# Queries turned whole two sequences ahead and stacked through DRAM, and the residual's load issued three exponentials later

## The chip, the cores and the metric

One core of a Trainium2 chip runs the kernel. The metric is the device time of one execution in microseconds; of several runs the median counts. The chip's engines run side by side and meet only at semaphores: TensorE (PE: matmuls, PEld: its weight loads), VectorE (DVE), ScalarE (ACT), GpSimd (POOL) and SyncE (SP). SyncE and ScalarE also issue the transfers (DMA), each from a queue of its own.

## The reference

64 sequences of 256 rows and 512 columns go through a cross-attention block and a gated mixing block. All is float32.

```python
def _L0_xattn_ref(q, k, v, ffn_w, ffn_b):           # 16 heads of 32
    qs = relu(q.reshape(bs, ts, h, hd)); ks = relu(...); vs = relu(...)
    att = einsum('bthf,byhf->bhty', qs, ks)
    att = softmax(att / sqrt(hd), axis=-1)
    out = einsum('bhty,byhf->bhtf', att, vs).reshape(bs, ts, -1)
    return relu(out @ ffn_w.T + ffn_b)

def _L0_ffn_ref(x, W_r, W_k, W_v, mu_r, mu_k):
    x_prev = concatenate([zeros, x[:, :-1]], axis=1)
    xr = mu_r * x + (1 - mu_r) * x_prev; xk = mu_k * x + (1 - mu_k) * x_prev
    r = sigmoid(xr @ W_r.T); k_act = square(relu(xk @ W_k.T))
    return r * (k_act @ W_v.T)

x = x + tanh(g_xattn[0]) * _L0_xattn_ref(layernorm(x), ctx, ctx, ffn_w, ffn_b)
x = x + tanh(g_ffn[0]) * _L0_ffn_ref(layernorm(x), W_r, W_k, W_v, mu_r, mu_k)
```

## The kernel before

A sequence is the unit of work. All weights stay in SBUF. Each engine has its own program, written out by hand: a function `iteration(i, par)` that lists its operations for sequence i and, beside them, those of i - 1, i - 2, i + 1 and i + 2, so that four sequences are under way at once. `pipeline` runs it for a few i as plain code, for most in a loop of two, and for the last ones plainly again. Within an engine this written order is the order of execution; waits on semaphores stand in the helpers.

**Precision.** A float32 operand is split into a high part (rounded to float32r) and a low part. Dense products take three matmuls (`product`, L951). Queries and keys are stacked for it: 96 partitions hold three parts of a head's 32 features, queries as high, high, low and keys as high, low, high, so that one matmul gives the whole score.

**Heads.** The 16 heads go in four groups of four, c = 0 to 3. For each head n, `scores` (L906) gives scores with queries down the partitions; VectorE takes each row's negated maximum (`head_max`, L699) into `m_nat`. When a group's four heads have theirs, `turn_m` (L884) turns them into `tp_bank`, `copy_m` (L708) copies them to `m_t`, and SyncE moves them (`move_m`, L279) as one row, partition 96, into `q_st`. `shifted_scores` (L918) then gives the scores the other way round with the maximum already taken off, ScalarE takes the exponential (`exponent`, L496) into `probs`, and `values` (L932) and `denominators` (L944) use them. The first shifted scores of a group wait for the group's row:

```python
if g == 0:
    pe.wait_ge(m_moved[c % 2], 16 * (2 * b + c // 2 + 1))
```

**Queries.** x is normalised in `x_ln`; ScalarE writes two high parts (`q_high`, L469 and L470) and VectorE the low part (`q_low`, L674) of a half of the sequence into `q_nat`. TensorE turns them, four heads of 96 columns at a time (`turn_q`, L875), and ScalarE copies each turn into `q_st` (`q_stack`, L477): eight turns and eight copies for a sequence.

**Keys.** They come turned from the host. `load_k` (L250) fetches those of i + 2; `k_halve` (L485) on ScalarE and `k_low` (L682) on VectorE split them; `write_k` (L258) writes both parts to `k_dram`, and `stack_k` (L270, L272) reads a group from there into `k_st`, in the next iteration.

**SyncE's queue.** It issues, in this order: `stack_k(i, 3)`, `store(i - 3)` (L301), `move_m(i, 1)`, `write_o`, `read_o` (L294: the attention's output through DRAM), `load_k(i + 2)`, `stack_k(i + 1, 0)`, `move_m(i, 2)`, and so on to `write_k(i + 2)`. A wait in it holds back all that follows.

**Residual.** `load_x1` (L453) brings x once more, into the buffer that `store` empties, so it waits for a store to have landed. ScalarE issues it between exponentials 1 and 2.

## Time and profile before

| | |
|---|---|
| median of 3 runs | 2981.95 us (2980.19 to 2983.81) |
| the profiled execution: its time, and its span | 2980.25 us, 2978.4 us |
| TensorE busy | 2860.3 us, 96% |
| VectorE, ScalarE, GpSimd busy | 2330.1, 1564.3, 1045.4 us |
| mean granted clock of TensorE | 0.993 of full |
| moved by DMA | 408.56 MB, mean 137 GB/s |
| busy share of the DMA engines: SyncE's queue, ScalarE's | 39.6%, 7.3% |

The span runs from the first to the last instruction. Busy time of TensorE is modelled from starts and shapes, so 96% says only that a matmul was under way. L numbers are lines of the kernel before.

### The profile page before, as it was taken

What the parts mean: (1) busy time and instruction counts of PE and PEld (TensorE: products, weight loads), DVE (VectorE), ACT (ScalarE), POOL (GpSimd) and SP (SyncE); (2) the same over time, 40 slices, a digit from 0 to 9 for tenths busy, and PEclk for the clock granted to TensorE, in tenths of its full rate; (3) what the DMA queues carried; (4) which work ended last, traced back from release to release, by engine and by line L of the source; (5) the groups of instructions that cost most, each with busy time, mean ns of one, the idle gap of its engine ahead of it and who ended that gap; (6) DMA issues with size and microseconds to landing.
All of it is one profiled execution on the core that took longest, in us unless ns stands there. A gap on an engine that the chain in (4) does not pass through costs nothing.

```text
span 2978.4 us, 71298 instructions
## 1 busy us (share of the span) xinstructions
PE 2860.3 (96%) x23168; PEld 2190.6 (74%) x23168; DVE 2330.1 (78%) x4175; ACT 1564.3 (53%) x2828; POOL 1045.4 (35%) x902
## 2 busy tenths in 40 slices
PE   3899999999999999999999999999999999999998
PEld 2677777777777777777777777777777777777776
DVE  5777877878878878878877877877878778788774
ACT  4445555555455455555555555555555555554552
POOL 0233333333343343333333333333333333333434
PEclk9899999999999999999999999999999999999999
DMA  5544445445445445445445445455455454454431
GB/s 168 150 122 140 144 124 155 140 127 155 135 131 156 137 131 154 133 137 150 131 142 149 128 143 153 120 149 152 120 152 146 124 152 142 124 156 137 130 109 41
DMA packets 405258, 408.56 MB, mean 137 GB/s; under 512 B 164577, under 2 KB 329441, under 8 KB 405218
## 3 DMA queue, kind: packets, MB, share of 16 engines
q1 hardware_dynamic: 352994, 340.92, 39.6%
q10 hardware_dynamic: 52224, 67.12, 7.3%
q8 instruction: 24, 0.39, 0.1%
q14 instruction: 16, 0.13, 0.0%
HBM read 272.64 MB, written 134.22 MB: 137 GB/s over the span
## 4 chain that ended last, share of the span: by engine, by line
PE 59%; DVE 16%; DMA 10%; SPq 7%; issue 5%; ACT 1%; ACTq 1%; DVEq 0%; POOL 0%; POOLq 0%
PE bank L951 29%; DMA out_dram<-x 8%; PE bank L918 7%; PE bank L932 6%; PE bank L906 5%; PE bank L944 4%; DVE m_nat L699 4%; DVE o_val L718 4%; SPq L272 3%; DVE st L652 3%; DVE k_raw L682 2%; PE bank L893 2%; PE bank L875 2%; SPq L258 2%; SPq L270 2%
## 5 line engine op out<-in xcount | busy, mean ns | idle before, releaser
L496 ACT ACTIVATE probs<-bank 128x512 f32<-128x512 f32 x1024 | 596.4, 594 | 455.7 <-PE bank L918 228.1
L699 DVE TENSOR_REDUCE m_nat<-bank 128x2 fp32r<-128x512 f32 x1024 | 695.4, 685 | 107.4 <-PE bank L906 106.7
L477 ACT ACTIVATE q_st<-bank 96x512 fp32r<-96x512 f32 x512 | 304.1, 594 | 718.9 <-PE bank L875 718.8
L918 PE MATMUL bank<-q_st,k_st 97*128 97x256 f32 x2048 | 449.9, 301 | 64.2 <-ACT probs L496 47.4
L718 DVE RECIPROCAL o_val<-bank 128x256 f32<-128x256 f32 x256 | 449.1, 1754 | 56.1 <-PE bank L944 51.7
L918 PEld LDWEIGHTS bank<-q_st,k_st 97*128 97x128 f32 x2048 | 341.8, 191 | 153.8 <-issue 58.5
L906 PE MATMUL bank<-k_st,q_st 96*128 96x256 f32 x2048 | 431.6, 293 | 7.4 <-DMA k_st<-k_dram 4.8
L397 POOL TENSOR_TENSOR xm<-xm 128x512 f32<-128x512 f32 x128 | 133.3, 1041 | 787.2 <-ACT xm L540 787.2
L906 PEld LDWEIGHTS bank<-k_st,q_st 96*128 96x128 f32 x2048 | 358.2, 192 | 59.8 <-issue 6.2
L708 DVE CAST m_t<-bank 4x256 fp32r<-4x256 f32 x256 | 105.1, 411 | 285.5 <-PE bank L884 285.4
L364 POOL TENSOR_TENSOR o_lo<-o_mv,o_hi 128x512 fp32r<-128x512 f32 x128 | 164.8, 1287 | 430.0 <-ACT o_hi L503 430.0
L951 PE MATMUL bank<-xk_hi,w_hi 128*128 128x256 f32 x1024 | 298.5, 292 | 0.0
L951 PE MATMUL bank<-xk_lo,w_hi 128*128 128x256 f32 x1024 | 286.5, 280 | 0.0
L951 PE MATMUL bank<-xk_hi,w_lo 128*128 128x256 f32 x1024 | 286.4, 280 | 0.0
L932 PE MATMUL bank<-probs,v_pos 128*32 128x256 f32 x4096 | 276.3, 388 | 0.6 <-DVE o_val L720 0.6
L944 PE MATMUL bank<-probs,ones_r 128*32 128x256 f32 x4096 | 276.3, 388 | 0.0
L875 PEld LDWEIGHTS bank<-ident_r,q_nat 128*96 128x96 f32 x2048 | 192.6, 127 | 71.0 <-issue 51.9
L875 PE MATMUL bank<-ident_r,q_nat 128*96 128x128 f32 x2048 | 218.6, 230 | 23.8 <-DVE q_nat L674 20.5
L382 POOL TENSOR_TENSOR xk_lo<-xm,xk_hi 128x512 fp32r<-128x512 f32 x128 | 164.5, 1286 | 215.0 <-ACT xk_hi L527 183.6
L356 POOL TENSOR_TENSOR rstd<-ve,mhalf 128x1 f32<-128x1 f32 x128 | 69.2, 541 | 422.8 <-DVE ve L736 422.8
L951 PE MATMUL bank<-w_hi,xr_hi 128*128 128x512 f32 x512 | 208.4, 407 | 4.2 <-POOL xr_lo L390 4.2
L951 PE MATMUL bank<-w_hi,o_hi 128*128 128x512 f32 x512 | 207.8, 406 | 4.7 <-POOL o_lo L364 4.7
(90 smaller groups left out, 6026.6 us busy)
## 6 DMA issues: line engine op xcount, KB each, us to landing
k_st<-k_dram SPq DMA_DIRECT2D x256, 256.0 KB, 3.6
k_raw<-ctx_t_dram SPq DMA_DIRECT2D x256, 128.0 KB, 3.0
x_ln<-x_dram SPq DMA_DIRECT2D x256, 128.0 KB
k_dram<-k_high SPq DMA_DIRECT2D x64, 512.0 KB, 3.0
k_dram<-k_raw SPq DMA_DIRECT2D x64, 512.0 KB, 4.5
k_st<-k_dram SPq DMA_DIRECT2D x256, 128.0 KB, 3.5
o_dram<-o_val SPq DMA_DIRECT2D x256, 128.0 KB, 1.7
o_mv<-o_dram SPq DMA_DIRECT2D x512, 64.0 KB, 2.2
```

Source lines behind the costliest of these rows:

```text
L364: nc.gpsimd.tensor_tensor(by_tile(o_lo, u), o_mv[:, :, :].rearrange("p g (k a) -> p k g a", k=KC), by_tile(o_hi, u).bitcast(F32), ALU.subt ...
L382: nc.gpsimd.tensor_tensor(xk_lo[:, part, :], xm[:, part, :], xk_hi[:, part, :].bitcast(F32), ALU.subtract).then_inc(xk_lo_ready, 1)
L477: nc.scalar.activation(q_st[0:QK, c, :, P * u:P * u + P], tp_bank[0:QK, :].rearrange("p (g t) -> p g t", g=GR), ACT.Copy).then_inc(q_stack ...
L496: nc.scalar.activation(probs[:, n // GR % 2, n % GR, :, :].rearrange("p v t -> p (v t)"), st_bank[n % 2][:, :], ACT.Exp, scale=SCALE).then ...
L699: nc.vector.tensor_reduce(m_nat[:, c % 2, :, n % GR:n % GR + 1], s_bank[n % 2][:, :].rearrange("p (u y) -> p u y", u=NU), AX_X, ALU.max, n ...
L718: nc.vector.reciprocal(o_val[:, :], pv_bank[:, T:2 * T]).then_inc(rden_ready, 1)
L875: mm = nc.tensor.transpose(tp_bank[0:QK, P * g:P * g + P].bitcast(F32R), q_nat[:, u, GR * c + g, :, :], ident_r[:, :])
L906: mm = nc.tensor.matmul(s_bank[n % 2][:, T * u:T * u + T], q_st[0:QK, c, g, P * u:P * u + P], k_st[0:QK, c, g, :], start=True, stop=True)
L918: mm = nc.tensor.matmul(st_bank[n % 2][:, T * v:T * v + T], k_st[0:ST, c, g, P * v:P * v + P], q_st[0:ST, c, g, :], start=True, stop=True)
L932: nc.tensor.matmul(pv_bank[HD * g:HD * g + HD, 0:T], v_pos[:, v, HD * h:HD * h + HD], probs[:, c % 2, g, v, :], start=(v == 0), stop=(v == ...
L944: mm = nc.tensor.matmul(pv_bank[HD * g:HD * g + HD, T:2 * T], ones_r[:, 0:HD].bitcast(F32), moving, start=(n == 0), stop=(n == len(sums) - 1))
L951: mm = nc.tensor.matmul(dst, lhs[a], rhs[c], start=first and n == 0, stop=last and n == 2)
```

## The change

It does four things.

- Queries of i + 2 are normalised by VectorE into `q_nat`, its columns reordered so that a group's features lie as (feature, head). TensorE turns them whole, not split: two turns of four 128-column blocks in plain float32. ScalarE copies each turn with a relu into `q_raw`, then rounds `q_raw` into `q_high`; VectorE subtracts.
- SyncE writes both parts to a new DRAM tensor `q_dram` and reads each group from there into `q_st`, three parts of 32 partitions, in two transfers a group, next to those of the keys.
- `load_x1` is issued between exponentials 4 and 5.
- x is loaded, and its statistics taken, three sequences ahead instead of two; the pipeline starts at i = -3.

```diff
+            def write_q(b, par):
+                if on(b):
+                    sp.wait_ge(q_hi_ready, b + 1)
+                    sp.wait_ge(q_lo_ready, b + 1)
+                    for half, tile in enumerate((q_high, q_raw)):
+                        sp.dma_start(q_dram[par, :, half].rearrange("c f g t -> (f g) c t"),
+                                     tile[:, :, :]).then_inc(q_written, 16)
+            def stack_q(b, c, par):
+                if on(b):
+                    sp.dma_start(q_st[0:HD, c, :, :].bitcast(F32), q_dram[par, c, 0]).then_inc(q_stacked[c], 16)
+                    sp.dma_start(q_st[HD:QK, c, :, :].bitcast(F32),
+                                 q_dram[par, c].rearrange("h f g t -> (h f) g t")).then_inc(q_stacked[c], 16)
...
             def iteration(i, par):
                 stack_k(i, 3, par)
+                stack_q(i, 3, par)
                 store(i - 3, 1 - par)
                 move_m(i, 1)
...
                 keys_written(i + 1)
                 load_k(i + 2)
+                queries_written(i + 1)
                 stack_k(i + 1, 0, 1 - par)
+                stack_q(i + 1, 0, 1 - par)
                 move_m(i, 2)
...
                 write_k(i + 2, par)
+                write_q(i + 2, par)
...
-            def q_stack(b, c, u):
+            def q_copy(b, u):
                 if on(b):
+                    act.wait_ge(q_turned, NU * b + u + 1)
+                    after(act, q_written, 32 * b)
+                    nc.scalar.activation(q_raw[:, :, P * u:P * u + P],
+                                         tp_bank[:, :].rearrange("p (c t) -> p c t", c=CH),
+                                         ACT.Relu).then_inc(q_copied, 1)
...
+            def turn_q(b, u, *users):
+                if on(b):
+                    pe.wait_ge(x_normed, NU * b + u + 1)
                     freed(*users)
+                    for c in range(CH):
+                        mm = nc.tensor.transpose(tp_bank[:, P * c:P * c + P], q_nat[:, u, c, :],
+                                                 ident_r[:, :].bitcast(F32))
                     mm.then_inc(q_turned, 1)
...
                 head_max(i + 1, 1)
+                q_low(i + 2)
```

SyncE's queue, from the end of one iteration into the next. Before:

```order
L258 DMA k_dram<-k_high 128x4x256
L258 DMA k_dram<-k_raw 128x4x256
L194 REGISTER_ALU
L270 DMA k_st<-k_dram 64x1024
L272 DMA k_st<-k_dram 32x1024
L300 REGISTER_ALU
L301 ISA
L301 DMA out_dram<-x 128x2x512
L278 REGISTER_ALU
L279 DMA q_st<-m_t 1x4x256
```

The same place with the change, from the last write of the keys on:

```order
L281 DMA q_dram<-q_high 128x4x256
L281 DMA q_dram<-q_raw 128x4x256
L199 REGISTER_ALU
L272 DMA k_st<-k_dram 64x1024
L274 DMA k_st<-k_dram 32x1024
L291 DMA q_st<-q_dram 32x1024
L292 DMA q_st<-q_dram 64x1024
L321 REGISTER_ALU
L322 ISA
L322 DMA out_dram<-x 128x2x512
L299 REGISTER_ALU
L300 DMA q_st<-m_t 1x4x256
```

Two writes and one pair of reads of the queries now stand between the writes of the keys and the store; the move of `m_t` follows the store in both.

ScalarE around the load of the residual, `x<-x_dram` (the exponentials are L496 before, L518 with the change). Before, from head 0 to head 2:

```order
L496 ACTIVATE probs<-bank 128x512
L489 REGISTER_ALU
L496 ACTIVATE probs<-bank 128x512
L474 REGISTER_ALU
L477 ACTIVATE q_st<-bank 96x4x128
L453 REGISTER_ALU
L453 DMA x<-x_dram 128x2x512
L489 REGISTER_ALU
L496 ACTIVATE probs<-bank 128x512
L540 ACTIVATE xm<-bank 128x512
```

With the change, from head 3 on:

```order
L518 ACTIVATE probs<-bank 128x512
L511 REGISTER_ALU
L518 ACTIVATE probs<-bank 128x512
L199 REGISTER_ALU
L480 REGISTER_ALU
L480 DMA x<-x_dram 128x2x512
L562 ACTIVATE xm<-bank 128x512
L492 REGISTER_ALU
L199 REGISTER_ALU
L494 ACTIVATE q_raw<-bank 128x4x128
L523 ISA
L525 ACTIVATE o_hi<-o_mv 128x4x128
```

The load of the residual stood ahead of the exponential of head 2 and now stands behind that of head 4, and the copies into `q_st` are gone from between.

## Rows read from the trace of the kernel before

**Rows 1.** The page: the span, and TensorE's busy time, share and instructions.

```profile
span 2978.4 us, 71298 instructions
...
PE 2860.3 (96%) x23168; PEld 2190.6 (74%) x23168; DVE 2330.1 (78%) x4175; ACT 1564.3 (53%) x2828; POOL 1045.4 (35%) x902
```

**Rows 2.** Waits from 500 to 2500 us: us in total, times, longest us.

```profile
ACT probs L496 <- DMA out_dram<-x: 158.4, 45, 3.8
...
PE bank L918 <- ACT probs L496: 32.4, 45, 1.0
```

**Rows 3.** The chain that ended last, one sequence: start, us, what.

```profile
1403.54 0.51 PE bank L918 x2
...
1409.15 0.21 PE bank L884 x2
...
1415.16 0.24 PE bank L918 x2
...
1430.46 0.23 PE bank L884 x2
...
1439.41 0.39 SPq L258
...
1443.08 4.14 DMA out_dram<-x
...
1448.63 0.47 PE bank L918 x2
```

**Rows 4.** Timeline of SyncE's queue: start us, us.

```profile
1402.57 1.87 SPq L294 DMA_DIRECT2D o_mv<-o_dram  x4
1404.73 2.85 SPq L250 DMA_DIRECT2D k_raw<-ctx_t_dram  x4
...
1440.46 1.01 SPq L270 DMA_DIRECT2D k_st<-k_dram  x1
...
1443.59 0.62 SPq L279 DMA_DIRECT2D q_st<-m_t  x1
```

**Rows 5.** Timeline of TensorE: in brackets the idle time before, and its releaser.

```profile
1448.63 0.47 PE L918 MATMUL bank<-q_st,k_st 97*128 97x256 f32 x2 [0.78 <-ACT probs L496]
```

**Rows 6.** Busy time by stretch, with PEclk, DMA share and GB/s at the end.

```profile
1397.00:1398.00 1.00, 1.00 (x11) 1.00 (x10) 1.00 (x1) 0.00 (x0) 0.00 (x0) 1.00 0.99 345
...
1404.00:1411.00 7.00, 7.00 (x61) 4.70 (x61) 3.49 (x6) 6.12 (x12) 4.27 (x4) 1.00 0.88 259
...
1440.00:1447.00 7.00, 7.00 (x75) 6.02 (x68) 6.77 (x12) 0.59 (x1) 0.00 (x0) 1.00 0.95 300
```

**Rows 7.** The chain again: products, and turns of queries (L875) and of xn (L893).

```profile
1415.40 0.70 PE bank L951 x3
...
1416.34 0.25 PE bank L875 x4
1416.59 0.76 PE bank L951 x3
...
1419.28 0.59 PE bank L893 x4
```

**Rows 8.** Groups by line: busy us, mean ns, idle before and releaser.

```profile
L477 ACT ACTIVATE q_st<-bank 96x512 fp32r<-96x512 f32 x512 | 304.1, 594 | 718.9 <-PE bank L875 718.8
...
L674 DVE SCALAR_TENSOR_TENSOR q_nat<-x_ln,q_nat 128x512 fp32r<-128x512 f32 x128 | 99.1, 775 | 108.1 <-ACT q_nat L470 108.1
...
L682 DVE SCALAR_TENSOR_TENSOR k_raw<-k_raw,k_high 128x1024 fp32r<-128x1024 f32 x64 | 79.1, 1236 | 0.0
```

**Rows 9.** Timeline of VectorE at the turn of 1430.46.

```profile
1430.80 0.41 DVE L708 CAST m_t<-bank 4x256 fp32r<-4x256 f32 x1 [2.07 <-PE bank L884]
```

**Rows 10.** An early standstill: timeline of TensorE, the stretch behind it, the chain.

```profile
182.74 0.47 PE L918 MATMUL bank<-q_st,k_st 97*128 97x256 f32 x2 [2.43 <-ACT probs L496]
...
183.42:186.83 3.41, 3.41 (x11) 2.75 (x11) 1.39 (x2) 3.41 (x8) 1.49 (x2) 0.50 1.13 306
...
183.71 1.28 PE bank L951 x3
```

More of the change, by code:

```diff
@@ L139, in flamingo_block @@
         q_turned = sem("q_turned")
-        q_stacked = sem("q_stacked")
+        q_copied = sem("q_copied")
+        q_written = sem("q_written")
+        q_stacked = [sem(f"q_stacked{c}") for c in range(CH)]
         v_ready = sem("v_ready")
@@ L207, in pipeline @@
         def pipeline(eng, iteration):
-            for i in range(-2, 4):
+            for i in range(-3, 4):
                 iteration(i, i % 2)
-            with eng.Fori(6, NB // 2 + 3) as pair:
+            with eng.Fori(6, NB // 2 + 2) as pair:
                 iteration(pair * 2 - 8, 0)
                 iteration(pair * 2 - 7, 1)
-            for i in range(NB - 2, NB + 3):
+            for i in range(NB - 4, NB + 3):
                 iteration(i, i % 2)
@@ L314, in iteration @@
                 stack_k(i + 1, 1, 1 - par)
-                load_x(i + 2)
+                stack_q(i + 1, 1, 1 - par)
+                load_x(i + 3)
                 move_m(i, 3)
@@ L318, in iteration @@
                 stack_k(i + 1, 2, 1 - par)
+                stack_q(i + 1, 2, 1 - par)
                 move_m(i + 1, 0)
@@ L580, in iteration @@
                 exponent(i, 4)
+                load_x1(i - 1, 1 - par)
                 kt_relu(i - 2, 1)
-                q_high(i + 1, 1)
+                q_copy(i + 2, 0)
                 o_high(i - 1, 1)
@@ L1059, in iteration @@
                 values(i - 1, 3)
-                turn(1)
+                turn(0)
                 denominators(i - 1, 3)
@@ L1064, in iteration @@
                 dense(0, 3)
-                turn(2)
                 shifted_scores(i, 2)
@@ L1072, in iteration @@
                 shifted_scores(i, 3)
-                turn(3)
                 dense(1, 2)
@@ L1081, in iteration @@
                 dense(2, 1)
+                turn(1)
                 shifted_scores(i, 5)
@@ L1099, in iteration @@
                 scores(i, 14)
-                turn(6)
                 dense(3, 3)
@@ L1105, in iteration @@
                 scores(i, 15)
-                turn(7)
                 dense(4, 1)
@@ L1119, in iteration @@
                 denominators(i, 1)
-                turn(10)
+                turn(6)
                 scores(i + 1, 1)
@@ L1127, in iteration @@
                 dense(5, 3)
-                turn(11)
                 shifted_scores(i, 12)
@@ L1137, in iteration @@
                 values(i, 2)
-                turn(12)
+                turn(7)
                 scores(i + 1, 4)
@@ L1145, in iteration @@
                 denominators(i, 2)
-                turn(13)
                 dense(7, 1)
```

100 lines of the change are left out of this document (39 added, 61 removed).

## The prediction, made before the changed kernel ran

> **What bounds the kernel now.** I read the engines' totals first, then who waits for whom in the steady part, then the chain that ended last, then the queue on that chain. The totals [rows 1] show TensorE busy for 2860.3 of 2978.4 us. That reads like a kernel bound by matmuls, but the busy figure says nothing of who sets the pace. The waits between 500 and 2500 us [rows 2] hold one odd entry: ScalarE waits 45 times, up to 3.8 us, for the store of an output to land, and L918 on TensorE waits 45 times for an exponential. Once in every sequence, then.
>
> The chain through one sequence [rows 3] shows why. Name the shifted scores of head 4 (L918, first of group 1) S4. They start at 1403.54 and, one sequence on, at 1448.63: a period of 45.09 us. Between them the chain goes in three legs:
> - A: TensorE from S4 to its turn of the maxima of the next sequence's group 0 (L884 at 1430.46): 26.92 us without a hole that counts.
> - B: VectorE from there through its statistics, a reciprocal and k_low (L682) until SyncE can issue write_k (L258) at 1439.41: 8.95 us, one operation behind the other, while TensorE runs ahead.
> - C: the queue of SyncE: write_k, stack_k, then the store at 1443.08, which lands 4.14 us later, at 1447.22. Only then can ScalarE issue load_x1 (L453) and go on to the exponential that S4 waits for.
>
> TensorE idled 0.78 us before S4 [rows 5], so it was ready at 1447.85. In leg C the DMA engines are full: 0.95 busy at 300 GB/s from 1440 to 1447, with no room in it [rows 6]. So leg C is a matter of bytes: 1 MB of keys, 384 KB of stacks, 512 KB of output. And behind the store in the same queue stands the move of m for group 1 (L279, issued at 1443.59) [rows 4]. It carries the row that S4 needs. The profile gives no landing for it; it is 4 KB behind the store in one queue, so I put it at the store's landing, 1447.2. It can't be later than 1448.63, or S4 would not have run.
>
> **The change on TensorE.** Per sequence, eight turns of four matmuls (L875) go, and two turns of the form of L893 come. In the chain a turn of L875 takes 0.25 us and slows the product behind it from 0.70 to 0.76 [rows 7]: 0.31 us, eight times 2.5. L893 takes 0.59 [rows 7], twice 1.2. TensorE gains 1.3 us. Where: two of the eight lie between k_low's end and S4, two more between the turn at 1430.46 and k_low's end, four in leg A. The two new ones lie both in leg A. So leg A keeps its length (4 x 0.31 against 2 x 0.59) but for 0.1 us of a wait for ScalarE that goes: 26.8 us. The gain is all before S4, where TensorE is ready at 1447.85 - 4 x 0.31 = 1446.6, and there it waits.
>
> **On ScalarE and VectorE.** ScalarE loses eight copies of 594 ns (L477) [rows 8] and the four halvings of q_high, and gets two copies of that size and one halving of twice the size: some 5 us of work less in 45. What it has left to do is waited for nowhere in the chain but behind the store, so nothing comes of that by itself. VectorE swaps two operations of 775 ns for one like k_low, 1236 ns [rows 8]. It stands after head_max(i + 1, 1), ahead of the turn at 1430.46, where VectorE idles 2.07 us [rows 9]; 1.24 us fits. If that cover were gone, leg B would start later by what exceeds it. Leg B's own operations stay as they are: 8.95 us.
>
> **load_x1 three exponentials later.** That takes the wait for the store away from ScalarE: the load now stands behind exponential 4, thus behind S4, when the store has long landed. But S4 then waits for the next thing in line, the row of m behind the same store. At an unchanged queue the period would be 26.8 + 8.95 + 7.8 (1447.22 less 1439.41) = 43.6 us, a gain of 1.5 us and no more.
>
> **What is put into the queue.** Per sequence two writes of 512 KB and four pairs of stacks of 384 KB: 2.5 MB. What counts is what stands ahead of the row of m. As the order of the queue shows, after write_k come both writes of q, and after stack_k(3) comes stack_q(3), all ahead of the store and of m. That is 1.05 + 0.39 = 1.44 MB in a stretch that is full already. At leg C's 300 GB/s it takes 4.8 us; at the pace of the fastest microsecond, 345 GB/s [rows 6], 4.2. I take 4.7, near the mean, since the mix is the same (1 KB pieces written, 4 KB read). Issuing costs nothing: the stack's issue takes 1.01 us and the move's 0.62 [rows 4], and four more of that size still run ahead of the bytes. A small extra: load_v, which stood behind ScalarE's wait, now falls into this stretch, 128 KB or 0.4 us; I leave that to the upper end. The Trainium skill (DMA: Bandwidth & Descriptors, Specifications) puts the limit of HBM for a core at about 358 GB/s. By that figure the 1.44 MB could not take less than 4.0 us, and the forecast would be 0.7 us a sequence lower; the stretch's own 300 GB/s is what I go by.
>
> **The rest of the queue.** The nearest danger is the row of m for group 2, issued behind read_o (1.87 us), load_k (2.85 us) [rows 4], stack_k(0) and now stack_q(0), 1.1 us each: about 7.5 us behind S4. Its turn (L884) comes 5.6 us behind S4 today [rows 3], about 6.2 with a new turn ahead of it. The DMA engines are 0.88 busy over the 7 us behind S4 [rows 6]; with 1.3 us for stack_q(0) that is 7.5 us of bytes, done by some 9.5 us behind S4, and the row by 10.5. The shifted scores of head 8 come 11.6 us behind S4 [rows 3], then 12.2. So no second wait, by under 2 us. The other two stacks of q fall behind that, where nothing is near.
>
> **The period after.** 26.8 + 8.95 + 7.8 + 4.7 = 48.3 us, against 45.1: +3.2. From 1430.46 TensorE needs 16.1 us until it is ready for S4, so it stands still for 48.3 - 26.8 - 16.1 = 5.4 us in every sequence.
>
> **The clock.** Early in this trace there is such a standstill: at 182.74 S4 starts after 2.43 us of idling [rows 10]. From 183.42 to 186.83 the granted clock is 0.50, the 1.2 GHz level, and three products take 1.28 us [rows 10] in place of 0.70 [rows 7]. Work at half the clock for 3.41 us loses 1.7 us. A standstill of 5.4 us should do that too. From below: nothing, if the clock held after all. From above: two such stretches, 3.4 us. I take one, 1.7, since one is what the row shows. The Trainium skill (TensorE: Matmul & The Clock Gate, What's actually happening) says that the throttled state is the default and that activity releases it; by that rule the fall comes back in every sequence that has the standstill, and by the row it came at least once.
>
> **The sum.** 3.2 + 1.7 = 4.9 us a sequence. A sequence has all of it when a later one's queries are written ahead of its row of m: all but the first and the last few, I count 61. 299 us. The few early sequences that stood and slowed before already had part of it, about -8. The longer fill (queries through DRAM before the first score) about +5, an estimate from the same legs. The profiled execution took 2980.25 us beside a span of 2978.4 [rows 1], within 2 us of the median 2981.95. 2980 + 299 - 3 = 3276; I say 3275.
>
> **Rivals.**
> - *Stall and clock as forecast*: 3185 to 3370, likeliest 3275. Chance 0.63.
> - *Stall, but the clock holds*: +3.2, or +2.7 with 4.2 us for the bytes: 2980 + 61 x 2.7 to 3.2 = 3145 to 3175. Against it: 182.74 [rows 10], a shorter standstill. Chance 0.15.
> - *More waits than that*: the margin at head 8 breaks, or there are two stretches of slow clock and load_v's bytes as well, 2 us more a sequence: 3275 + 122 = 3397 and up. Chance 0.08.
> - *Faster: the row of m isn't held up.* If it lands before TensorE is ready, TensorE itself is the period: 26.8 + 16.1 = 42.9 us, 2.2 less, 61 times 134: 2845. If it still waits for the store as today, 43.6: 61 x 1.5 = 92 less, 2890. Either needs the added bytes to pass beside the others, or m's few pieces to pass them. From 1.5 us of added delay on nothing is left (43.6 + 1.5 = 45.1), and I count 4.7. For it: 1.3 us of matmuls and a wait of up to 3.8 us [rows 2] really go. Against: DMA engines without room in this stretch [rows 6]. Chance 0.11.
> - *The two cancel*, within 0.2% (6 us): needs just this 1.5 us. Chance 0.03.
>
> 0.2% is about what a measurement of this kernel tells from no change. Slower: 0.63 + 0.15 + 0.08 = 0.86; same 0.03; faster 0.11. The range goes from 3140 (bytes at their fastest, no slow clock) to 3375 (the bytes at their slowest and load_v's with them, 3.3 + 0.4, and most of a second slow stretch, 2.8: 6.5 x 61 = 395); that leaves out the fast case and the worst one, some 0.2.
>
> **What would show it.** L918's idle time before S4 put down to the move of m (q_st<-m_t), 4 to 6 us, once a sequence; the wait of ScalarE for out_dram gone; DMA full for about 12 us in a row after k_low; the granted clock at half for a few us behind each S4; S4 to S4 near 50 us. TensorE's busy share falls from 96% [rows 1] to below 90%, though it has less to do. Wrong would be: S4 unwaited and a period near 43; or the bytes of q gone through in under 2 us; or a new wait elsewhere, on scores for q_st or in the products for o_hi.

## The result, and the profile after

The changed kernel takes 3377.32 us (median of 4 runs, 3374.70 to 3382.67), against 2981.07 us (4 runs, 2977.55 to 2983.81) for the kernel before on the same chip: 1.133 times, 95% interval 1.131 to 1.135. That is 396 us more, where the forecast had 293. It lies 2 us above the top of the range.

The page of the changed kernel, to be held against [rows 1]. In the lines of its groups stand busy us, mean ns, then idle us ahead and its releaser:

```profile
span 3376.4 us, 66228 instructions
...
PE 2912.3 (86%) x21632; PEld 2220.3 (66%) x21632; DVE 2396.3 (71%) x4111; ACT 1329.0 (39%) x2252; POOL 1042.2 (31%) x902
...
L933 PE MATMUL bank<-q_st,k_st 97*128 97x256 f32 x2048 | 471.3, 314 | 325.5 <-DMA q_st<-m_t 325.5
```

TensorE has 86% where 96% stood, and 325.5 us of idling before one line: L933, which was L918 before, put down to the move of m. Yet its busy time is longer than before though it does less: part of it runs at half the clock. The waits between 500 and 2900 us (us in total, times, longest us):

```profile
ACT probs L518 <- PE bank L933: 1094.3, 563, 8.1
...
PE bank L933 <- DMA q_st<-m_t: 227.0, 47, 5.2
...
PE bank L921 <- DVE m_nat L716: 38.1, 47, 0.9
```

Once a sequence TensorE stands for the row of m, 4.8 us on average, where it stood 45 times for an exponential [rows 2]. ScalarE's wait for the store is gone. New besides is that TensorE waits for VectorE's maxima, 0.8 us a sequence before the scores of head 10 (the last line) and 0.3 us before their turn (L899: 15.2 us, 47 times); the kernel before has neither wait in its steady part. S4 is found early and late in TensorE's timeline, in brackets the idle time before it:

```profile
428.62 0.80 PE L933 MATMUL bank<-q_st,k_st 97*128 97x256 f32 x2 [5.14 <-DMA q_st<-m_t]
...
2527.61 0.79 PE L933 MATMUL bank<-q_st,k_st 97*128 97x256 f32 x2 [4.70 <-DMA q_st<-m_t]
```

There are 41 sequences between them: 51.2 us each. The store of an output gives the same count more handily, since SyncE issues it once a sequence. The row of all 64 (ns, then start of the first and of the last):

```profile
L322 SPq DMA_DIRECT2D out_dram<-x x64: 400/406/592, 217.7 to 3373.1; - x64
```

In the kernel before they start at 175.2 and 2975.1. From the seventh to the 57th it takes 2560.1 us after (524.83 to 3084.97) and 2249.9 before (453.73 to 2703.66): 51.20 and 45.00 us a sequence. So of the 398 us between the two spans 42 fall before the first store, and the rest is 6.2 us a sequence. One sequence in the chain that ended last (start us, us, what), beside [rows 3]:

```profile
1498.12 5.40 DMA q_st<-m_t
1503.64 0.79 PE bank L933 x2
...
1504.86 1.28 PE bank L966 x3
...
1507.85 0.85 PE bank L890 x4
...
1532.39 0.23 PE bank L899 x2
...
1540.06 1.22 DVE k_raw L699
...
1545.39 0.74 SPq L272
1546.17 1.33 SPq L274
...
1549.44 5.01 DMA q_st<-m_t
1554.49 0.80 PE bank L933 x2
```

The products behind S4 take 1.28 us for three, the half-clock price, in place of 0.70 [rows 7]. The chain ends in the queue, as forecast. SyncE's timeline at that place (start us, us of issuing), against [rows 4]:

```profile
1541.35 0.39 SPq L260 DMA_DIRECT2D k_dram<-k_high  x1
...
1542.39 0.99 SPq L281 DMA_DIRECT2D q_dram<-q_high  x1
1543.44 1.30 SPq L281 DMA_DIRECT2D q_dram<-q_raw  x1
...
1547.54 0.46 SPq L291 DMA_DIRECT2D q_st<-q_dram  x1
...
1548.92 0.41 SPq L322 DMA_DIRECT2D out_dram<-x  x1
1549.44 0.66 SPq L300 DMA_DIRECT2D q_st<-m_t  x1
```

From write_k's issue at 1541.35 to S4 at 1554.49 are 13.14 us. In that stretch, from ScalarE's queue, falls also the transfer of load_v, 128 KB:

```profile
1545.70 0.39 ACTq L486 DMA_DIRECT2D v_pos<-ctx_dram  x1
```

Two stretches of the same kernel, the first over the full DMA engines, the second over the slow clock (PEclk, DMA share and GB/s are the last three columns):

```profile
1542.00:1554.00 12.00, 7.17 (x64) 6.08 (x64) 9.42 (x15) 1.69 (x3) 1.24 (x1) 0.98 0.99 303
1553.60:1560.40 6.80, 5.91 (x19) 5.03 (x20) 0.69 (x1) 1.85 (x4) 1.04 (x1) 0.50 0.71 197
```

The DMA engines are full for 12 us at 303 GB/s, the pace the forecast took from [rows 6]. And the clock stands at 0.50, the 1.2 GHz level, for 6.8 us around S4: twice the 3.41 us of the early standstill [rows 10]. All 47 slow stretches between 500 and 2900 us are that long, one in each sequence.

### The profile page after: what moved, and what is told of

The parts are those of the page before. It is cut to its first block, busy times and chain, and to the rows that moved or that the text cites. A ratio compares the mean times of both kernels' runs of the same rounds, so it can differ in the third digit from the quotient of the medians.

```text
span 3376.4 us, 66228 instructions
## 1 busy us (share of the span) xinstructions
PE 2912.3 (86%) x21632; PEld 2220.3 (66%) x21632; DVE 2396.3 (71%) x4111; ACT 1329.0 (39%) x2252; POOL 1042.2 (31%) x902
## 4 chain that ended last, share of the span: by engine, by line
PE 61%; DVE 15%; DMA 11%; SPq 8%; issue 4%; DVEq 0%; POOL 0%; ACT 0%; POOLq 0%; ACTq 0%
PE bank L966 31%; DMA q_st<-m_t 10%; PE bank L933 7%; PE bank L959 6%; PE bank L947 6%; PE bank L921 5%; DVE m_nat L716 4%; DVE o_val L735 3%; SPq L274 3%; PE bank L890 2%; DVE k_raw L699 2%; DVE st L667 2%; PE bank L908 2%; PE bank L899 2%; SPq L272 1%
## 5 line engine op out<-in xcount | busy, mean ns | idle before, releaser
L518 ACT ACTIVATE probs<-bank 128x512 f32<-128x512 f32 x1024 | 610.1, 596 | 1501.4 <-PE bank L933 1501.2
L933 PE MATMUL bank<-q_st,k_st 97*128 97x256 f32 x2048 | 471.3, 314 | 325.5 <-DMA q_st<-m_t 325.5
L933 PEld LDWEIGHTS bank<-q_st,k_st 97*128 97x128 f32 x2048 | 379.0, 207 | 412.3 <-DMA q_st<-m_t 198.5
L921 PE MATMUL bank<-k_st,q_st 96*128 96x256 f32 x2048 | 450.8, 303 | 61.3 <-DVE m_nat L716 54.6
L921 PEld LDWEIGHTS bank<-k_st,q_st 96*128 96x128 f32 x2048 | 374.1, 200 | 134.1 <-DVE m_nat L716 68.9
L424 POOL TENSOR_TENSOR xm<-xm 128x512 f32<-128x512 f32 x128 | 146.5, 1145 | 973.9 <-ACT xm L562 973.9
L966 PE MATMUL bank<-w_hi,o_hi 128*128 128x512 f32 x512 | 240.9, 471 | 3.4 <-POOL o_lo L391 3.4
L966 PE MATMUL bank<-w_hi,o_lo 128*128 128x512 f32 x512 | 232.9, 455 | 0.0
L966 PE MATMUL bank<-w_lo,o_hi 128*128 128x512 f32 x512 | 230.0, 449 | 0.0
L966 PEld LDWEIGHTS bank<-xk_hi,w_hi 128*128 128x128 f32 x1024 | 193.3, 189 | 26.0 <-issue 25.9
L966 PE MATMUL bank<-w_hi,ka_hi 128*128 128x512 f32 x512 | 210.1, 410 | 0.0
```

What stands on the lines that cost most here:

```text
L424: nc.gpsimd.tensor_tensor(part, part, part, ALU.mult).then_inc(ka_ready, 1)
L518: nc.scalar.activation(probs[:, n // GR % 2, n % GR, :, :].rearrange("p v t -> p (v t)"), st_bank[n % 2][:, :], ACT.Exp, scale=SCALE).then ...
L921: mm = nc.tensor.matmul(s_bank[n % 2][:, T * u:T * u + T], q_st[0:QK, c, g, P * u:P * u + P], k_st[0:QK, c, g, :], start=True, stop=True)
L933: mm = nc.tensor.matmul(st_bank[n % 2][:, T * v:T * v + T], k_st[0:ST, c, g, P * v:P * v + P], q_st[0:ST, c, g, :], start=True, stop=True)
L966: mm = nc.tensor.matmul(dst, lhs[a], rhs[c], start=first and n == 0, stop=last and n == 2)
```

## The experiments

"After" is the changed kernel. The table has for each the median in us and its runs; the ratio to the kernel before on the same chip, with its 95% interval; from its profile the start of the first store and the time of a sequence (seventh to 57th store, over 50), in us; and the mean granted clock.

| | us | ratio | first store | a sequence | clock |
|---|---|---|---|---|---|
| before | 2981.07 (2977.55 to 2983.81) | | 175.2 | 45.00 | 0.993 |
| after | 3377.32 (3374.70 to 3382.67) | 1.133 (1.131 to 1.135) | 217.7 | 51.20 | 0.934 |
| e1 | 3066.05 (3060.74 to 3072.55) | 1.028 (1.026 to 1.030) | 207.4 | 46.07 | 0.977 |
| e2 | 3276.49 (3266.31 to 3289.66) | 1.101 (1.097 to 1.105) | 212.4 | 49.31 | 0.961 |
| e3 | 3258.49 (3252.00 to 3263.53) | 1.093 (1.091 to 1.095) | 214.4 | 49.08 | 0.993 |
| e4 | 2936.17 (2933.43 to 2938.08) | 0.985 (0.983 to 0.987) | 178.1 | 44.38 | 0.997 |
| e5 | 3017.12 (3013.74 to 3020.28) | 1.013 (1.011 to 1.014) | 201.2 | 45.31 | 0.994 |
| e6 | 3380.92 (3379.38 to 3381.07) | 1.135 (1.133 to 1.137) | 217.6 | 51.20 | 0.932 |
| e7 | 2945.99 (2942.17 to 2951.82) | 0.990 (0.988 to 0.991) | 172.0 | 44.59 | 0.997 |
| e8 | 3406.80 (3400.76 to 3409.46) | 1.143 (1.141 to 1.145) | 220.3 | 51.69 | 0.929 |
| e9 | 3382.58 (3380.59 to 3388.88) | 1.136 (1.134 to 1.138) | 215.5 | 51.19 | 0.933 |
| e10 | 2919.54 (2917.95 to 2925.01) | 0.981 (0.979 to 0.982) | 203.9 | 43.59 | 0.994 |
| e11 | 2889.29 (2888.49 to 2890.71) | 0.970 (0.969 to 0.971) | 173.5 | 43.64 | 0.996 |
| e12 | 3438.24 (3431.12 to 3443.88) | 1.154 (1.151 to 1.156) | 218.3 | 52.24 | 0.978 |
| e13 | 2936.01 (2935.18 to 2940.07) | 0.986 (0.984 to 0.987) | 202.5 | 43.87 | 0.993 |
| e14 | 2940.32 (2927.69 to 2955.68) | 0.987 (0.985 to 0.990) | 206.2 | 43.85 | 0.991 |
| e15 | 3149.14 (3141.69 to 3152.47) | 1.058 (1.056 to 1.059) | 207.3 | 47.34 | 0.993 |

The prediction's three legs, measured in the traces: A from S4 to the start of the turn of the maxima, B from there to the issue of write_k, C from there to the next S4. These are means in us over 48 sequences, from the ninth's S4 to the 57th's. The fourth column is TensorE's idle time right before S4, the last when the store of the output lands, counted from the issue of write_k (in the queue it stands ahead of the row of m for group 1, except in e10 and e11).

| | A | B | C | idle before S4 | store landed |
|---|---|---|---|---|---|
| before | 26.82 | 9.03 | 9.15 | 0.72 | 7.80 |
| after | 28.71 | 9.03 | 13.47 | 4.83 | 13.39 |
| e1 | 27.06 | 9.03 | 9.98 | 1.34 | 10.07 |
| e3 | 26.71 | 9.02 | 13.35 | 0.63 | 13.35 |
| e6 | 28.16 | 9.02 | 14.01 | 6.15 | 12.65 |
| e8 | 27.98 | 9.02 | 14.71 | 6.07 | 14.52 |
| e9 | 28.76 | 9.03 | 13.40 | 4.77 | 13.34 |
| e10 | 26.09 | 9.03 | 8.48 | 0.00 | 10.74 |
| e11 | 26.35 | 9.03 | 8.27 | 0.00 | 8.40 |
| e15 | 26.67 | 9.03 | 11.65 | 0.17 | 11.61 |

**Where the bytes stand: e1, e9, e15.** e1 is after with both writes of q ahead of write_o(i, 2) and write_k:

```diff
                 read_o(i, 0)
+                write_q(i + 2, par)
                 write_o(i, 2)
                 write_k(i + 2, par)
-                write_q(i + 2, par)
```

> The changed kernel with the two writes of the queries issued ahead of write_o(i, 2), where the DMA engines are idle, instead of behind write_k. Nothing else differs. Theory (what counts is the bytes that stand ahead of the row of m for group 1): 1.05 MB or 3.4 us leave the stretch, so the row lands 9.7 us behind write_k instead of 13.1, the standstill before S4 shrinks to some 2.6 us, a part of the clock's loss goes too. Period 45.5 to 47 us against 51.2; 3377 less 61 x 4.2 to 5.7 = 3030 to 3120 us. Rival A (the sum of bytes or contention counts, wherever they lie): no change, 3377. Rival B (the turns in plain float32 or the new work on other engines cost the time): no change either.

Measured 3066.05 us, inside the expected 3030 to 3120. The same 1 MB, no byte fewer, costs 311 us less from two places further up, 5.1 us a sequence. What is left of the standstill, between 500 and 2700 us:

```profile
PE bank L933 <- DMA q_st<-m_t: 63.2, 48, 1.7
```

e9 puts in a spare write of 512 KB a sequence that nobody reads, away from that place:

```diff
                 load_x(i + 3)
+                write_spare(i)
                 move_m(i, 3)
```

> The same write of 512 KB, issued behind load_x(i + 3), where the DMA engines are nearly idle. Theory: no row that TensorE waits for stands close behind it: 3377 within 15 us. Rival (total of bytes, contention): as much slower as the run with the write ahead of the row, some 3480.

Measured 3382.58 us, at an unchanged 51.19 us a sequence. But the place was not free: the row of m for group 3 stands behind the spare write, and TensorE now waits for it too, 0.7 us a sequence before the shifted scores of head 12 (500 to 2700 us, where after has 43 waits):

```profile
PE bank L944 <- DMA q_st<-m_t: 233.7, 82, 5.1
```

Leg A is as long as in after even so (28.76 and 28.71 us), because less of the slow clock falls into it: 3.9 us behind S4 in place of 5.7. So the even time is in part luck, and e9 alone does not show that bytes aside cost nothing. What shows that the place in the queue counts and not the total is e1, with e10 below, which moves all of after's bytes at 43.59 us a sequence. e15, below, gives the price of 512 KB ahead of the row.

**The clock: e3.** After, with 34 matmuls more ahead of S4's wait; they write a bank that S4 writes over. They keep TensorE at work while it waits, and change nothing in the queue.

```diff
+                    after(pe, exp_ready, HEADS * b + n - 1)
+                    if n == GR:
+                        for _ in range(34):
+                            nc.tensor.matmul(st_bank[n % 2][:, 0:T], k_st[0:QK, c, g, 0:P], q_st[0:QK, c, g, :], ...)
                     if g == 0:
                         pe.wait_ge(m_moved[c % 2], 16 * (2 * b + c // 2 + 1))
-                    after(pe, exp_ready, HEADS * b + n - 1)
```

> The changed kernel with 34 extra matmuls of 96x128 by 256 columns, about 4 us, between the exponential's wait and the wait for the row of m ahead of S4; they write a bank that S4 then overwrites. They fill most of the standstill. Theory: the row of m lands as before, but the clock stays at its upper level, and what the products behind S4 lose (about 2 us a sequence) comes back: 3377 - 61 x 2.0 = 3255 us, granted clock near 0.99 instead of 0.934. Rival (the clock's fall costs nothing more, since the row of m sets the pace anyway, or TensorE's own work bounds the kernel): 3377, or 3377 + 61 x 4 = 3620 if TensorE bounds it.

Measured 3258.49 us, where 3255 was expected. More work, 119 us less, the mean clock back at 0.993, and no slow stretch between 500 and 2900 us. The chain of this kernel shows S4 at 1497.60, SyncE's timeline the next write_k at 1532.99, TensorE's timeline the next S4:

```profile
1546.34 0.50 PE L937 MATMUL bank<-q_st,k_st 97*128 97x256 f32 x2 [0.63 <-DMA q_st<-m_t]
```

Leg C is still 13.35 us, in this sequence and on average, and still ended by the row of m. What went is the half clock, 2.1 us a sequence (51.20 less 49.08): 2.0 in leg A, 0.1 in leg C.

**The price of 512 KB with the clock up: e15.** As e3 (24 matmuls), and write_q issues one half at a time: the high half of q written early, the low half where the change has both:

```diff
                 read_o(i, 0)
+                write_q(i + 2, par, 0)
                 write_o(i, 2)
                 write_k(i + 2, par)
-                write_q(i + 2, par)
+                write_q(i + 2, par, 1)
```

> The changed kernel with the high part of the queries written early (behind read_o(i, 0)) and only the low part behind the keys, and 24 extra matmuls (2.8 us) that keep the clock up. Against the run with 34 extra matmuls (3258 us) it takes 512 KB away from ahead of the row of m, at the upper clock in both. Theory: 1.7 us a sequence: 3258 - 61 x 1.7 = 3155 us. If the place of 512 KB is worth only what the spare write showed where the clock falls: 3230.

Measured 3149.14 us, 109 less than e3, and 1.74 us a sequence less, of which leg C has 1.70. The forecast's rate (4.7 us for 1.44 MB) gives 1.7 for 512 KB.

**512 KB more ahead of the row: e8, e12.** After with the spare write of e9 behind write_q instead.

```diff
                 write_k(i + 2, par)
                 write_q(i + 2, par)
+                write_spare(i)
```

> The changed kernel with one more write of 512 KB a sequence to a spare tensor in DRAM, behind the writes of q, so ahead of the row of m. Theory: 512 KB at about 308 GB/s is 1.7 us: 3377 + 60 x 1.7 = 3480 us, period near 52.9. If it is the total of bytes that costs, the run with the same write elsewhere in the sequence slows as much.

Measured 3406.80 us, 29 more than after, 0.49 us a sequence. The row comes later, TensorE stands 6.3 us at the longest in place of 5.2; but as many bytes cost 1.74 us a sequence in e15. The clock's record says where part of the rest is. In one sequence of after, ahead of S4 and from it on:

```profile
1553.60:1554.40 0.80, 0.00 (x0) 0.00 (x0) 0.00 (x0) 0.00 (x0) 0.00 (x0) 0.50 0.65 229
1554.40:1560.40 6.00, 5.91 (x19) 5.03 (x20) 0.69 (x1) 1.85 (x4) 1.04 (x1) 0.50 0.72 193
```

The same of one sequence of e8, where S4 starts at 1520.31:

```profile
1517.00:1520.30 3.30, 0.00 (x0) 0.00 (x0) 0.00 (x0) 0.00 (x0) 0.00 (x0) 0.50 0.85 273
1520.30:1523.50 3.20, 3.19 (x10) 2.71 (x11) 0.23 (x1) 1.19 (x2) 0.99 (x1) 0.50 0.36 92
```

In this sequence of e8 half of the slow stretch passes while TensorE stands, and only 3.2 us of work are slow in place of 6.0. These two lie far apart. On average 4.1 us of slow clock follow S4 in e8 and 5.7 in after; leg A is 0.73 us shorter and leg C 1.24 longer, which leaves the 0.5. So the row comes 1.24 us later here where e15 gives 1.70 for as many bytes; that difference of 0.5 us no run explains.

e12 was to show that without the clock: e8 with 48 matmuls of e3's kind.

```diff
+                write_spare(i)
...
+                        for _ in range(48):
```

> The spare write of 512 KB ahead of the row of m again, now with the extra matmuls (48 of them, about 5.6 us) that keep the clock up through the standstill. Theory: the write delays the row by 1.7 us a sequence in both cases, and where the clock falls, the fall covers it, since the slow stretch is over at its own time and a later S4 runs less work in it. So here the write shows its whole price: 3258 + 61 x 1.7 = 3360 us, against 3258 with the extra matmuls alone. Rival (the write isn't worth 1.7 us at this place, the DMA engines take it in beside the rest): 3258 to 3290, as it was 29 us where the clock falls.

Measured 3438.24 us, 180 over e3, or 3.2 a sequence. It missed its 3360 by 78, and its time can't be read as a price of bytes: the mean clock is 0.978, with 19 slow stretches between 500 and 2900 us, and S4 comes 16.5 us behind write_k after only 0.17 us of idling, so it is the added matmuls, and not the row, that hold TensorE there. The store ahead of the row lands 14.90 us behind write_k, 1.55 later than in e3, which is near the 1.7 expected of the bytes.

**The residual's load alone: e4, e6.** e4 is the kernel before with load_x1 behind exponent(i, 4), nothing else.

```diff
-                load_x1(i - 1, 1 - par)      # behind exponent(i, 1)
...
                 exponent(i, 4)
+                load_x1(i - 1, 1 - par)
```

> The kernel before with load_x1 issued behind the exponential of head 4; nothing of the queries is changed. Theory: ScalarE's wait for the store goes; the row of m lands with the store, 0.6 us ahead of the moment at which TensorE is ready, so TensorE sets the pace: 26.8 + 17.4 = 44.2 us against 45.0; 2981 - 61 x 0.8 = 2930 us. Rival (the row of m lands later than the store, since more stands in the queue than I can see): S4 waits for m_t, and the time stays at 2981.

Measured 2936.17 us, 45 less than before: this part of the change gains by itself. The prediction had 1.5 us a sequence for it at an unchanged queue; it is 0.62, as TensorE itself sets the pace: S4 follows write_k by 8.28 us without a wait, and not by 7.8, and leg A is 27.07 us. What takes the place of the wait, between 500 and 2700 us:

```profile
PE bank L951 <- POOL o_lo L364: 23.8, 50, 1.6
```

TensorE stops for the low part of the attention's output, 0.5 us a sequence.

e6 is after with the load back at its old place.

```diff
                 exponent(i, 1)
                 split_high(i, 0)
+                load_x1(i - 1, 1 - par)
...
                 exponent(i, 4)
-                load_x1(i - 1, 1 - par)
```

> The changed kernel with load_x1 back behind the exponential of head 1. Theory: the store lands with the row of m, then ScalarE needs 1.1 us more (issue, exponential) before S4 can start: period up by about 1 us, 3377 + 60 = 3440 us, and S4 waits for ScalarE instead of the move. Rival (the load's new place is what costs): below 3377.

Measured 3380.92 us. The wait moved as expected (500 to 2700 us):

```profile
ACT probs L518 <- DMA out_dram<-x: 573.8, 43, 13.5
...
PE bank L933 <- ACT probs L518: 264.9, 43, 6.3
```

The time did not follow: 4 us, not 60, with the same 51.20 us a sequence. S4 comes 0.54 us later behind write_k, and leg A is 0.55 us shorter: as in e8, TensorE's standstill is longer (6.3 us at most), and more of the slow clock falls into it. The run shows one thing more. With the load at its old place, load_v too is issued late, 13.6 us behind write_k in place of 4.4, and without its 128 KB the store lands at 12.65 us in place of 13.39.

**The row ahead of the stacks: e2, e7, e5.** e2 is after with move_m(i, 1) first in the iteration:

```diff
+                move_m(i, 1)
                 stack_k(i, 3, par)
                 stack_q(i, 3, par)
                 store(i - 3, 1 - par)
-                move_m(i, 1)
```

> The changed kernel with move_m(i, 1) issued at the head of the iteration, ahead of both stacks of group 3 and the store; the writes of q stay behind those of the keys. Same bytes, same operations. Theory: only the 2.1 MB of the writes (6.9 us) stand ahead of the row, it lands about 8.4 us behind write_k, TensorE is ready at 7.2; a standstill of 1.2 us, no fall of the clock. Period 26.8 + 9.0 + 8.4 = 44.2 us; 3377 - 61 x 7.0 = 2950 us, if the scores of head 12 don't wait for their keys and queries, which now land only just in time. Rivals A and B (total bytes; turns): 3377.

Measured 3276.49 us, a miss by 326. The expected part happened, S4 stands no more, though it comes 8.5 us behind write_k and not 7.2; the waits between 500 and 2900 us show what took its place:

```profile
ACT xm L562 <- DMA out_dram<-x: 201.5, 49, 4.6
...
ACT o_hi L525 <- DMA o_mv<-o_dram: 173.2, 49, 4.1
...
PE bank L966 <- POOL o_lo L391: 152.6, 49, 3.7
```

The bytes are not gone, only overtaken. Behind them stand the store that ScalarE now waits for and the read of the attention's output, which it turns into o_hi and GpSimd into o_lo, and TensorE stands for that, 3.1 us a sequence.

e7 does the same to e4, where no bytes of q exist.

```diff
+                move_m(i, 1)
                 stack_k(i, 3, par)
                 store(i - 3, 1 - par)
-                move_m(i, 1)
```

> The kernel before with load_x1 behind the exponential of head 4 and move_m(i, 1) at the head of the iteration. Theory: with load_x1 moved alone TensorE was waited for by nobody but itself (2936 us), so the earlier row brings nothing: 2936 within 15 us. If the row of m still held S4 a little there, some 10 to 30 us less; if the later store and o_mv make new waits, as they did in the changed kernel, up to 60 us more.

Measured 2945.99 us, 10 more than e4. Moving the row up is worth nothing where it is not late.

e5 joins e1 and e2.

```diff
+                move_m(i, 1)
                 stack_k(i, 3, par)
...
-                move_m(i, 1)
...
+                write_q(i + 2, par)
                 write_o(i, 2)
                 write_k(i + 2, par)
-                write_q(i + 2, par)
```

> Both orders together: the writes of q ahead of write_o(i, 2), and move_m(i, 1) at the head of the iteration. Theory: only the keys' 1 MB stands ahead of the row, it lands about 5 us behind write_k, TensorE is ready at 7.2: no standstill by the row. The run with move_m first alone had ScalarE wait 4.1 us a sequence for the store (at the load of the residual) and 3.5 for o_mv; with 3.4 us of bytes gone from ahead of them most of both goes. Period 43 to 44 us, 2880 to 2940 us: below the kernel before. If instead the turns in plain float32 or the sum of bytes cost the time, it stays above 3000.

Measured 3017.12 us. Better than each alone, by 49 and 259 us, and still 77 over what was expected. The waits between 500 and 2700 us:

```profile
ACT o_hi L525 <- DMA o_mv<-o_dram: 154.8, 48, 3.5
...
PE bank L966 <- POOL o_lo L391: 58.2, 48, 1.7
PEld bank L933 <- DMA q_st<-m_t: 22.9, 42, 1.1
```

The second line is read_o again; the third is the row of m for group 2 (head 8), the margin of "under 2 us" that the prediction named, now broken by stack_q(0) ahead of it.

**The whole queue in order: e10, e11.** The transfers put by when their readers need them: the row of m for group 1 first, write_o(i - 1, 3) ahead of the store, the row for group 2 ahead of the stacks of the next group 0, the writes of q ahead of write_o(i, 2) and write_k.

```diff
             def iteration(i, par):
+                move_m(i, 1)
                 stack_k(i, 3, par)
                 stack_q(i, 3, par)
+                write_o(i - 1, 3)
                 store(i - 3, 1 - par)
-                move_m(i, 1)
-                write_o(i - 1, 3)
                 read_o(i - 1, 1)
                 keys_written(i + 1)
                 load_k(i + 2)
+                move_m(i, 2)
                 queries_written(i + 1)
                 stack_k(i + 1, 0, 1 - par)
                 stack_q(i + 1, 0, 1 - par)
-                move_m(i, 2)
...
                 read_o(i, 0)
+                write_q(i + 2, par)
                 write_o(i, 2)
                 write_k(i + 2, par)
```

e10 is after with this order (and the load two operations later). e11 is the kernel before with this order, less what it has not (stack_q, write_q), and e4's load.

> The changed kernel with SyncE's queue in the order in which the rows are waited for: move_m(i, 1) first, write_o(i - 1, 3) ahead of the store, move_m(i, 2) ahead of the stacks of the next group 0, the writes of q behind read_o(i, 0); load_x1 two operations later, behind q_copy. Same operations and bytes as the changed kernel. Theory (place in the queue is all that was wrong with the change): the waits left in the run with both orders (the row for group 2, o_mv, the store) go, TensorE sets the pace at 42.9 us, 61 x 8.3 less than 3377: 2870 to 2900 us, below the kernel before and below it with load_x1 moved alone (2936). Rival (the bytes as such hold something up wherever they stand): 2960 or more.

> The kernel before, its queries turned split as they were, with the same order of SyncE's queue and the same late load_x1. It parts the worth of the order from that of the turns. Theory: TensorE's own work is 44.2 us a sequence here (eight turns of q against two longer ones), 1.3 more than in the changed kernel: 2930 to 2945 us, so 45 to 75 above the changed kernel in that order.

Measured 2919.54 us for e10, 20 above its expectation, and 2889.29 for e11, 41 below. Both beat the kernel before, and e11 is the fastest of all that were run. One stretch of e10:

```profile
500.00:2600.00 2100.00, 2043.57 (x16294) 1558.96 (x16293) 1787.68 (x3083) 986.74 (x1684) 782.16 (x674) 1.00 0.69 205
```

And of e11:

```profile
500.00:2600.00 2100.00, 2099.94 (x17418) 1630.64 (x17417) 1791.89 (x3126) 1174.06 (x2118) 781.97 (x677) 1.00 0.48 144
```

In e11 TensorE never stands, by its busy time as modelled: only now is the kernel bound by its matmuls. In e10 it has 56 us less to do in this stretch, 1.2 us a sequence, near the forecast's 1.3 for the unsplit turns. But it idles for all of it, and all but 2 us of that goes to waits for VectorE's maxima, before scores and before their turn (500 to 2600 us):

```profile
PE bank L921 <- DVE m_nat L716: 39.1, 48, 0.9
...
PE bank L899 <- DVE m_nat L716: 15.7, 49, 0.3
```

So a sequence takes as long with either way of turning, 43.59 and 43.64 us. The 30 us between the two lie ahead of the first store. These are its rows in e10, and in e11:

```profile
L322 SPq DMA_DIRECT2D out_dram<-x x64: 394/411/435, 203.9 to 2912.9; - x64
```

```profile
L301 SPq DMA_DIRECT2D out_dram<-x x64: 395/399/647, 173.5 to 2884.4; - x64
```

**Two tries at e10's wait: e13, e14.** In e13 VectorE's mix_r(i - 2) goes behind head_max(i, 8), in e14 ScalarE's kt_relu(i - 2, 0), and with it GpSimd's squaring, behind exponent(i, 3).

```diff
-                mix_r(i - 2)                 # e13
                 split_low(i, 0)

                 head_max(i, 8)
+                mix_r(i - 2)
...
-                kt_relu(i - 2, 0)            # e14
...
                 exponent(i, 3)
+                kt_relu(i - 2, 0)
```

> The changed kernel in the new order, with mix_r(i - 2) on VectorE behind head_max(i, 8) instead of ahead of it. In the run with the new order TensorE waits 0.9 us a sequence for that maximum, at the scores of head 10, and the chain there goes from the turn of group 0 through VectorE alone. Theory: that wait is all that keeps the unsplit turns from paying: 2919 - 61 x 0.9 = 2865 us, below the kernel before in the new order (2889). Rival (VectorE's chain only shifts, to the scores of head 11 or 12): 2905 to 2920.

> The run with the new order again, with kt_relu(i - 2, 0) on ScalarE behind the exponential of head 3 instead of that of head 2. GpSimd's squaring starts when that relu is done, and in the changed kernel and in the new order it falls onto VectorE's mix_r, of whose four operations one then takes 1.26 us instead of 0.48. Theory: the squaring leaves mix_r alone, L778 is back at 0.48 us on average, VectorE's chain is 0.8 us shorter, TensorE's wait at the scores of head 10 mostly goes: 2919 - 61 x 0.8 = 2870 us. Rival (something else slows that operation, or the squaring only falls onto the next one in the same chain): 2910 or more.

Measured 2936.01 and 2940.32 us, 16 and 21 more than e10. Both missed. In e13 (500 to 2600 us) the wait of L921 for m_nat halves, and another comes up:

```profile
PE bank L966 <- POOL o_lo L391: 26.9, 26, 1.9
...
PE bank L921 <- DVE m_nat L716: 20.0, 48, 0.5
```

In e14 the wait of L921 all but goes (2.6 us in total), and the same other one takes its place:

```profile
PE bank L966 <- POOL o_lo L391: 34.8, 30, 2.4
```

So close behind the maxima lies a second limit, the attention's output on its way through DRAM, o_hi and o_lo: ScalarE waits 129.2 us for its read in e14 and 119.8 in e13, against 52.1 in e10. Why these moves delay it stays open.

## Why the prediction was wrong

The direction, the place and the chain of causes were right; the size was not.

**Right.** S4 waits for the row of m, 47 times between 500 and 2900 us. ScalarE's wait for the store is gone. Leg B is 8.96 us in the sequence shown (turn of the maxima at 1532.39, write_k at 1541.35) against 8.95. The bytes of q at that place are the cause: e1 and e10 show the place, e15 the rate. The clock falls with the standstill, and e3 takes it away alone. The rival in which the clock holds falls with after's 6.8 us at 0.50, the one in which the bytes pass beside the others with the 12 full microseconds.

**Wrong, by its own steps.** Forecast and measured spans are 102 us apart (299 - 8 + 5 = 296 us above before, and 398). Three quarters of it are the period, 51.20 us where the forecast's terms make 50.0; the rest is the fill.

- *Leg C, 7.8 + 4.7 = 12.5 us.* It is 13.35 in e3, where the clock holds, and 13.47 in after. The 7.8 is right (the store lands at 7.80 before), and so is the rate, as e15 shows for 512 KB. What was left out is load_v: "I leave that to the upper end". ScalarE issues it 4.4 us behind write_k in every sequence, where before it came at 8.9, behind the store's landing. It was certain to come and belonged in the sum. Sized at 0.4, it is worth 0.74 by e6, where it comes late again and the store lands at 12.65, near the 12.5. This is the larger half of the period's error, 0.8 us.
- *"I take one, 1.7, since one is what the row shows."* The slow stretch is as long as two of those, 6.8 us in every sequence, and what it costs is 2.1 us (after less e3). That is 0.4 over the 1.7 and well under the 3.4 of the upper bound. Of the difference 0.6 is for the 1.2 us of the stretch that pass while TensorE stands; the rest no run splits up. A standstill of 2.43 us was the measure for one of 5.
- *The period.* 0.8 and 0.4 are the 1.2 between 50.0 and 51.20. From the 45.00 us that the kernel before has on average, and not the 45.09 of one sequence, the forecast was 1.3 short: 77 us over 59 sequences.
- *The fill.* The first store starts 42.4 us later than before. The forecast had 5 for the fill and, since it counted 61 sequences, two of 4.9 in that place: 15. This is 28 us, the rest of the miss. The 5 had no row behind it. TensorE's first scores (L921 at 44.16, L906 at 28.72 before) are already 15.4 us late, waiting for q_st from q_dram; S4 of the first sequence is 22.7 us late (79.2 against 56.5), and the others are lost in the three sequences up to the first store. Most of it comes with the queries' new way, one iteration more ahead included, and not with the order of the queue: in e10, where no sequence stands for the row of m for group 1, the first store is still 30.4 us later than in e11.

77 + 28 is 105; the early sequences that stood before anyway (-8 forecast, 48.3, 47.6 and 47.7 us from store to store against 45.0, so -8.6) and the end make up the difference. The range's top, 6.5 us a sequence, did hold the steady part, and not the fill.

**Near by luck.** The forecast had a standstill of 5.4 us, and it is 4.8. But two errors oppose each other there. The row comes 1.0 us later than forecast, and TensorE is ready 1.6 us later: 17.7 us behind the turn of the maxima (9.03 + 13.47 - 4.83) in place of 16.1, hardly other than the 17.5 before. So the step "the gain is all before S4, where TensorE is ready at 1446.6" failed: what the turns save there goes into the waits for VectorE's maxima, 0.8 + 0.3 us. In after this costs nothing, since TensorE stands there anyway. It is what keeps the gain from e10, and the expectations of e2, e5 and e10 were too low by building on it.

**Not thought of.** The order in the queue. e11 is 89 us below before; the late load alone has 45 of it (e4), so the order has about as much again, without any change of the queries. And after gains 458 us by it (e10, which has the load two operations later besides). By the prediction's numbers TensorE needs 42.9 + 1.3 = 44.2 us a sequence with split turns; e11 runs at 43.64.

## What to carry to other kernels

A transfer that nobody waits for still has a price: the time of its bytes, if a small transfer that somebody does wait for stands behind it in the queue, here 1.7 us per 512 KB in every sequence. Before a route through DRAM is added, write the queue down in the order of need; that and a late load gave 3% on the kernel before, about half each, and turned the change from 13% slower to 2% faster. Put every transfer that is certain to fall into a full stretch into the sum, whichever queue issues it. When a change makes TensorE's standstill longer than any in the trace, the slow stretch can be longer too, and only the part of it that meets work costs time: here 6.8 us cost 2.1. Follow the fill by its own legs.

## What the runs showed of the hardware

**The slow stretch does not begin with the work.** In after it begins 1.2 us before S4 on average, in e6 2.4, in e9 3.0 and in e8 3.2, and it ends 5.7, 4.4, 3.9 and 4.1 us behind it. After, e6 and e9 differ in what TensorE waits for and how long, and take 51.20, 51.20 and 51.19 us a sequence, since what comes on in one leg goes from the slow work in another. With the clock up, 512 KB move the period by 1.74 us. How the place of the slow stretch is set no run here tells.

**The same issue takes longer at another place.** SyncE issues the two writes of q in 1.00 and 1.30 us on average in after, where they follow the two writes of keys at once, and in 0.40 and 0.51 us in e10, where they come first. L272 and L274, the stacks of keys behind them, take 1.26 and 1.33 us in the sequence shown. The prediction had issuing at nothing; whether it delays the row no run separates.

**VectorE and GpSimd get in each other's way.** L778 and L769 on VectorE are of one shape. Their groups between 500 and 2600 us in e10, the first mean over 192:

```profile
L778 DVE SCALAR_TENSOR_TENSOR xd<-xd,mu_sb,xt 128x256 f32<-128x256 f32 x192 | 117.5, 673 | 0.0
...
L769 DVE SCALAR_TENSOR_TENSOR xm<-xd,mu_sb,xt 128x256 f32<-128x256 f32 x192 | 80.0, 480 | 0.0
...
L685 DVE TENSOR_SCALAR q_nat<-x_ln,mv,rstd 128x512 f32<-128x512 f32 x96 | 62.2, 730 | 0.0
```

L778's median is 477 ns and its longest 1270. In each of the 48 sequences of this stretch a squaring of GpSimd (L424) starts while one L778 runs. The L778 that follows takes 1.26 to 1.27 us, and the squaring 1.23 to 1.29, where the other one of the sequence, of the same shape, takes 1.04. In e14 the squaring comes later, and the same lines read:

```profile
L778 DVE SCALAR_TENSOR_TENSOR xd<-xd,mu_sb,xt 128x256 f32<-128x256 f32 x192 | 79.8, 477 | 0.0
...
L685 DVE TENSOR_SCALAR q_nat<-x_ln,mv,rstd 128x512 f32<-128x512 f32 x96 | 76.5, 880 | 0.0
```

The 0.8 us went from L778 and 0.3 us a sequence came to L685 instead: 17 of the 96 take 1.5 us and the others 0.7 to 0.75. So these two engines meet at more than semaphores, against what the opening says of all of them. The Trainium skill (SBUF — State Buffer, Who interferes with whom) says that a VectorE instruction with two inputs in SBUF and a GpSimd one that reads SBUF exclude each other for the whole instruction, and that the one that starts second waits. The rows agree for L778, whose two inputs are in SBUF. L685 is slower after than its counterpart before too, 730 against 539 ns; it writes its columns reordered, but no run separates that from the rest.
